# GpSimd's indirect transfers in rows of at most four, and one group's root and two tiles' scatters moved

## What is computed

```python
x = _layernorm(x + _L0_attn_ref(x, L0_attn_w_qkv, L0_attn_w_conv1), axis=-1)
x = _layernorm(x + _L0_ffn_ref(x, L0_ffn_gate_w, L0_ffn_W1, L0_ffn_W2, L0_ffn_Ws1, L0_ffn_Ws2), axis=-1)
# in _L0_ffn_ref, D = 256, H = 192, E = 8 experts, K = 2 per token:
scores = jax.nn.softmax((xf @ gate_w.T).astype(jnp.float32), axis=-1)
top_vals, top_idx = jax.lax.top_k(scores, K)
...
h = jnp.einsum('td,ehd->teh', xf, W1)
y, g = jnp.split(h, 2, axis=-1)
eo = jnp.einsum('teh,edh->ted', y * jax.nn.silu(g), W2)
z = jnp.einsum('te,ted->td', w_dense, eo)
z = z + _gated_mlp(xf, Ws1, Ws2)
```

## Time and profile before

| | us |
|---|---|
| median of 3 runs | 339.32 |
| lowest and highest run | 338.72, 341.7 |
| profiled execution | 339.15 |
| its span, first to last instruction | 337.4 |
| mean granted clock of TensorE | 0.98 of full speed |

### The profile page before, as it was taken

One profiled execution on the slowest core, in us unless ns is written; L12 is line 12 of the kernel. 1 busy time (PEld: TensorE's weight loads), 2 busy tenths in 40 slices (PEclk: granted clock), 3 DMA queues, 4 the chain that ended last, 5 costly groups with the idle time before them and its releaser, 6 DMA issues.

```text
span 337.4 us, 7796 instructions
## 1 busy us (share of the span) xinstructions
PE 311.0 (92%) x2190; PEld 277.4 (82%) x2190; DVE 266.3 (79%) x1083; ACT 194.8 (58%) x442; POOL 205.2 (61%) x241
## 2 busy tenths in 40 slices
PE   3889799999999999999999999999999999999960
PEld 2456688769798879888889999999999999998850
DVE  2795679865888898885789877776799889998686
ACT  1045686637374646465445666666655588688473
POOL 5049650746768776875757544447576856868760
PEclk9979999899999999999999999999999999999996
DMA  7977420211192111153257544447988988876953
GB/s 227 374 257 258 149 65 0 85 48 65 67 254 70 65 65 67 66 159 119 97 159 249 153 152 131 139 140 166 241 234 218 226 208 198 234 219 182 354 198 124
DMA packets 31383, 54.63 MB, mean 162 GB/s; under 512 B 4880, under 2 KB 22544, under 8 KB 31344
## 3 DMA queue, kind: packets, MB, share of 16 engines
q1 hardware_dynamic: 23136, 29.82, 28.5%
q0 software_dynamic: 8208, 24.32, 25.6%
HBM read 29.73 MB, written 24.40 MB: 160 GB/s over the span
## 4 chain that ended last, share of the span: by engine, by line
PE 54%; DVE 17%; DMA 9%; POOL 8%; ACT 5%; issue 3%; SPq 2%; DVEq 0%; ACTq 0%
PE bank L1129 19%; PE bank L1163 10%; PE bank L1012 8%; POOL rows_in L596 4%; PE bank L1093 4%; DMA stage<-ws_t 4%; PE bank L1036 4%; PE bank L996 3%; DMA x<-rows_out 2%; POOL w1lo L552 2%; PE bank L1143 2%; DVE htlo L1468 2%; DVE xs L1259 2%; DVE mix L1462 2%; DMA rows_in<-x,slot 2%
## 5 line engine op out<-in xcount | busy, mean ns | idle before, releaser
L654 POOL DMA_INDIRECT rows_out<-stage,place x71 | 69.8, 983 | 49.0 <-ACT stage L831 32.5
L596 POOL DMA_INDIRECT rows_in<-x,slot x64 | 64.6, 1009 | 47.0 <-DVE slot L1374 30.5
L1129 PE MATMUL bank<-w1hi,bx 128*128 x284 | 64.0, 346 | 0.2 <-DVE bx L1483 0.2
L1129 PEld LDWEIGHTS bank<-w1hi,bx 128*128 128x128 f32 x284 | 48.3, 188 | 0.7 <-issue 0.7
L811 ACT ACTIVATE stage<-bank 128x384 f32<-128x384 f32 (+1 forms) x36 | 17.5, 487 | 36.6 <-PE bank L1129 36.5
L831 ACT ACTIVATE stage<-bank,weight 128x256 f32<-128x256 f32 x71 | 30.0, 470 | 11.0 <-PE bank L1163 9.5
L1129 PE MATMUL bank<-w1lo,bx 128*128 x142 | 36.3, 336 | 0.0
L1483 DVE TENSOR_TENSOR bx<-bank,bx 128x512 fp32r<-128x512 f32 (+1 forms) x36 | 24.5, 684 | 13.5 <-ACT bx L753 13.1
L1036 PE MATMUL bank<-ws2hi,hthi 128*128 128x256 f32 x96 | 28.7, 299 | 5.0 <-DVE htlo L1468 3.3
L1012 PE MATMUL bank<-xthi,ws1hi 128*128 128x512 f32 x96 | 31.6, 411 | 0.0
L1012 PE MATMUL bank<-xthi,ws1lo 128*128 128x512 f32 x96 | 30.5, 400 | 0.0
(11 more groups left out here) (251 smaller groups left out, 871.9 us busy)
## 6 DMA issues: line engine op xcount, KB each, us to landing
stage<-rows_in SPq DMA_DIRECT2D x71, 133.0 KB, 2.6
xs<-rows_out POOLq DMA_DIRECT2D x12, 512.0 KB, 6.1
xs<-x SPq DMA_DIRECT2D x8, 512.0 KB, 8.3
out<-xs SPq DMA_DIRECT2D x7, 512.0 KB
stage<-w_t SPq DMA_DIRECT2D x8, 384.0 KB, 3.9
rows_in<-clear SPq DMA_DIRECT2D x16, 133.0 KB
rows_out<-stage,place POOLq DMA_INDIRECT x71
stage<-w_t SPq DMA_DIRECT2D x2, 512.0 KB, 3.9
```

The costliest lines, as they stand in the source:

```text
L596: pool.indirect_dma_start(rows_in[0:E * CAP, :], bass.IndirectOffsetOnAxis(slot[:, q * G + t, k:k + 1], 0), x2[q % 2][:, t, :], None).then ...
L654: pool.indirect_dma_start(rows_out[:, :], bass.IndirectOffsetOnAxis(place[:, 2 * j + b:2 * j + b + 1], 0), by[j % 4][:, b * C:(b + 1) * C] ...
L1129: mm = pe.matmul(bank_h[j % 2][:, b, 0:F], bx[j % 2][:, (2 * b + k) * P:(2 * b + k + 1) * P], w[:, bass.ds(e, 1), k, :], start=(a == 0), s ...
```

## The change

Scatters are issued by a helper, two transfers for a tile. In each group two tiles are scattered, then comes something else, then the other two: in groups 0 to 5 the root of group q + 2 (as before in groups 1 to 5; in group 0 it stood behind all eight), in group 6 a wait for the first half of the group's shared result (`s_zev[0]`). In group 7 only tiles 28 and 29 are scattered there; tile 30's two transfers come behind pair 0's results and tile 31's behind pair 2's. In the pair loop `rough_rstd2` of pairs 21, 27 and 31 moves from ahead of the pair's first transfer to behind it.

```diff
+            def scatter(q, t):
+
+                for k in range(K):
+                    pool.indirect_dma_start(
+                        rows_in[0:E * CAP, :], bass.IndirectOffsetOnAxis(slot[:, q * G + t, k:k + 1], 0),
+                        x2[q % 2][:, t, :], None).then_inc(s_sc[q % 2], 16)
+
             for q in range(NG):
                 pool.wait_ge(s_slot, q + 1)
-                for t in range(G):
-                    if t == 2 and 0 < q < NG - 2:
-                        rough_rstd(q + 2)
-                    for k in range(K):
-                        pool.indirect_dma_start(
-                            rows_in[0:E * CAP, :], bass.IndirectOffsetOnAxis(slot[:, q * G + t, k:k + 1], 0),
-                            x2[q % 2][:, t, :], None).then_inc(s_sc[q % 2], 16)
-                if q == 0:
-                    rough_rstd(2)
-                elif q < 5:
+                for t in range(2):
+                    scatter(q, t)
+                if q < NG - 2:
+                    rough_rstd(q + 2)
+                elif q < LAST:
+                    pool.wait_ge(s_zev[0], q + 1)
+                if q < LAST:
+                    for t in range(2, G):
+                        scatter(q, t)
+                if 0 < q < 5:
                     low(5 + q)
...
             for j in range(PAIRS):
                 if j % 2 == 0:
                     pool.wait_ge(s_to, j // 2 + 1)
-                if j in ROUGH:
-                    rough_rstd2(ROUGH[j])
...
                     pool.indirect_dma_start(
                         rows_out[:, :], bass.IndirectOffsetOnAxis(place[:, 2 * j + b:2 * j + b + 1], 0),
                         by[j % 4][:, b * C:(b + 1) * C], None).then_inc(s_st[j % 4], 16)
+                    if b == 0 and j in ROUGH:
+                        rough_rstd2(ROUGH[j])
+                if j in (0, 2):
+                    scatter(LAST, 2 + j // 2)
```

## The result

The changed kernel takes **346.22 us** (median of 4 runs, 344.49 to 348.89), the kernel before, run beside it, 340.51 us (338.72 to 343.9): a ratio of **1.019**, 95% interval [1.0137, 1.0243]. In two later series, each beside runs of the kernel before, the same change gave 1.0163 [1.0114, 1.0212] and 1.0173 [1.0122, 1.0224]. So it is slower, by 1.6 to 1.9%, or 5.7 to 6.6 us. Forecast were 344.7 us, 5.4 us or 1.6% above the 339.32 us shown, with a range up to 346.9; two of the four runs, 347.37 and 348.89, lie above it.

The account below looks back on a forecast made before the run. The prediction took TensorE to bound the kernel, busy in 92% of the span and without slack in the pair loop. Stall 3.5, clock 1.5 and root 0.5 make 5.5 us; 339.15 + 5.5 gives 344.7 us, range 341.7 to 346.9.

Parts of the forecast that it names:

- the sign: Whole kernel: the change makes it slower, beginning at 342.7 us; chance 0.87.
- the mechanism: Pair 8's loads wait for all 64 scatters, tile 31's included, so TensorE idles and its clock falls.
- the clock's term: Behind the gap at pair 8, TensorE's clock falls to 1.2 GHz: 1.5 us lost, bounds 0 and 1.7.
- the stall: At pair 8's transposes, TensorE idles from 194.7 to 198.2 us: 3.5 us, bounds 2.5 and 5.2.
- the root: In pair 31, the moved root delays the second transfer by 0.8 and the end by 0.5 us, bounds 0 and 0.8.
- TensorE has no slack in the pair loop: From 187 to 304 us TensorE is busy 117.00 of 117.00 us, so a pause is not made up later.
- pause given back: Rival: the pair loop's 27 steps behind the stall run faster and recover it, giving 339.7 us; chance 0.05.
- The pair loop delays tile 31 to 190.95 and 192.22: On GpSimd, tile 31's two scatters stand behind pair 2's transfers, the last 12.0 us later than before.
- 2.6 + 0.1 + 0.7 + 2.6 = 6.0 us: Before pair 8's transposes: scatter landing 2.6, SyncE's waits 0.1, second load 0.7 later, load landing 2.6 us.
- Groups 0 and 6 cost 0: Group 0's moved root costs 0 (bounds -0.2 and +1.04 us); group 6's wait on GpSimd costs 0.
- shorter rows of scatters help: Rival: no stall, at best 0.2 us gained from the first root, giving 339.0 us; chance 0.04.
- a stall without the fall: Rival: TensorE stalls at pair 8 but its clock does not fall, giving 343.2 us; chance 0.25.

Follow-up runs that it names:

- after_third: The changed kernel run again, unedited, in a later series: 346.4 us, ratio 1.0163 to the kernel before.
- filled_gap_2: The changed kernel with 60 matmuls of unread result ahead of pair 8's transposes: 343.71 us, ratio 1.0108 to the kernel before.
- g7_only_2: The kernel before with only tiles 30 and 31 deferred behind pairs 0 and 2: 346.21 us, ratio 1.0159 to the kernel before.
- t31_pair3: The changed kernel with tile 31 scattered behind pair 3 instead of pair 2: 350.63 us, ratio 1.0287 to the kernel before.
- after_fourth: The changed kernel run again, unedited, in another later series: 346.32 us, ratio 1.0173 to the kernel before.
- g7_undone_2: The changed kernel with group 7 scattered whole, the rest of the change kept: 340.62 us, ratio 0.9998 to the kernel before.
- g0g6_only: The kernel before with only groups 0 and 6 cut in two, no deferral and no roots moved into the pairs: 340.75 us, ratio 0.9993.
- before_again: The kernel before, unedited, profiled on a chip where it takes 356.6 us in the series: 354.85 us.

## Where the prediction was right, and the step of it that failed

It had the sign, the place and the mechanism. **The step that failed is the clock's term:** 1.5 us, with 1.7 as the upper bound, "0.4 of the 3.4 us lies in the gap". The profile after shows 6.8 us at the lower level, 5.4 of them under work, an estimated 2.7 us; and a second fall near the end, for which the sum had no term. Two smaller terms were mis-sized as well, the stall (3.5 for 3.6 to 3.8) and the root (0.5 for 0.3). The median, 346.22, is 1.5 us above the forecast 344.7, and the profiled execution, 348.89, is 2.0 above the range's upper end; 2.85 of its microseconds lie ahead of everything that changed. The forecast ratio, 344.7 / 339.32 = 1.016, is close to the three measured, 1.019, 1.0163 and 1.0173, in part by luck: 0.5 of the 5.5 us is a term that no time shows, and the others were short by as much or more. Its steps:

- *TensorE has no slack in the pair loop.* Right: 99.00 of 99.00 busy behind the gap; the rival "pause given back" is out.
- *The pair loop delays tile 31 to 190.95 and 192.22.* Measured 191.31 and 192.58 in after_third, 0.36 later; that run began group 7 0.5 us later (first scatter at 171.84, not 171.32).
- *From the last scatter's start to the transposes 2.6 + 0.1 + 0.7 + 2.6 = 6.0 us.* Measured 201.05 - 194.61 = 6.4: landing 2.48, SyncE's first load 0.36 behind it where I had estimated 0.1, the second 0.84 later where I chose 0.7 against the row's 0.85, landing 2.71. **The stall**, forecast 3.5, was 3.81, 3.71 and 3.6: short by 0.1 to 0.3, and it was in my two choices that lay at no row. The stall's upper bound was wrong by its own terms: 192.22 + 2.64 + 0.1 + 0.85 + 3.9 is 199.7, so 5.0 and not 5.2, and the range's end 346.7; the changed kernel's own stalls on this kind of chip, 3.6 to 3.8, stay far below it.
- **The clock**, forecast 1.5. That it falls is shown by every profile of the changed kernel, and what the fall costs by filled_gap_2, which takes it away: 1.8 us in the profile's middle row, 2.6 between the medians. I had put the place of the fall, in the gap, together with a length, 3.4 us, from a row in which TensorE was at work. In the five profiles with the stall these two don't go together:

| run | stall | fell at | TensorE resumed | at the lower level | of it at work | lost (estimate) |
|---|---|---|---|---|---|---|
| after | 3.81 | 199.6 | 201.05 | 6.8 | 5.4 | 2.7 |
| g7_only_2 | 3.60 | 198.7 | 200.32 | 6.8 | 5.2 | 2.6 |
| t31_pair3 | 7.13 | 200.0 | 202.41 | 6.8 | 4.5 | 2.2 |
| after_third | 3.71 | 200.3 | 198.94 | 3.4 | 3.4 | 1.7 |
| after_fourth | 3.61 | 200.1 | 198.90 | 3.4 | 3.4 | 1.7 |

Where the clock fell in the gap it stayed low twice as long; where it fell behind the gap, all of the 3.4 us were under work. Neither case gives 1.5. What decides between them isn't shown. My upper bound, 1.7, was none: a low stretch of 6.8 us stands in no row that I had read. The first and last microseconds of one, g7_only_2:

```profile
198.00:199.00 1.00, 0.00 (x0) 0.00 (x0) 0.00 (x0) 0.00 (x0) 0.65 (x1) 0.86 0.77 263
...
205.00:206.00 1.00, 1.00 (x8) 0.92 (x7) 0.16 (x1) 0.65 (x2) 0.00 (x0) 0.73 0.72 165
```

- **A second fall near the end**, in no term. All five of these profiles have it, beginning at 329.8 to 333.1 and for 3.4 us; of the five others of this kind of chip one has one (g7_undone_2, 322 to 325). From pair 10 to the end the six with it take 117.4 to 118.1 us, of the four without it three 116.6 to 116.9 and g0g6_only 118.2. So it may cost most of a microsecond; that, and whether the stall brings it about, was not tested.
- **The root in pair 31**, forecast 0.5. The transfer behind it moved as worked out: 306.53 to 316.10 is 9.57, against 8.75 for the pair's results (303.63 to 312.38), so 0.82. SyncE's loads behind it moved by less than the 0.5: they go out 6.30 to 6.32 us after pair 31's results begin in the seven profiles with the move, 5.97 to 5.99 in the three without, so 0.3. The chain that ended last now runs through the root, in after:

```profile
314.84 1.06 POOL ln2t L627
316.10 2.51 DMA rows_out<-stage,place
318.69 0.38 SPq L480
```

But nothing shows that the 0.3 us reached the end. The time from pair 10 to the end was, over the ten profiles of this kind of chip, 116.8 (before) to 118.2 us (g0g6_only) without the move and 116.6 (filled_gap_2) to 118.1 (after_third) with it. The landing of `load_last`'s rows, 7.31 us in the profile I read, was 8.08 in after and 8.87 in g0g6_only, so it hides them.
- *Groups 0 and 6 cost 0.* Right where the kernel takes 340 us (0.9993). The rival "shorter rows of scatters help" I priced at 0.2 us from the even pitch on GpSimd. That reading was right for the chip of the profile and wrong as a general one: on one chip of the other kind each cut gave half a per cent, on another the change without the deferral 1.3%, by what isn't shown.

So of the sum, 5.0 us were meant for the middle row of the table, and three profiles of the changed kernel show 5.5 to 6.2 there: 0.1 to 0.3 of the difference is the stall's, 0.2 to 1.2 the clock's. The chance of 0.25 for a stall without the fall went to a case that none of those profiles showed.

## What to carry to other kernels

Before you move a DMA behind later work, look for the semaphore that counts *all* of its kind, not for the tile that it carries: here one wait counts 64 scatters, so pair 8's load waits for the last of them, whichever rows it carries. Work out the last start that is still free (here 188 us: wanted at 194.7, less two landings and two issues) and put the work ahead of it. When a full TensorE gets a gap such as this one, add what its clock loses behind the gap, take it from several falls rather than one, don't combine the place of one with the length of another, and keep the longest in the range. And take a gain of half a per cent from one chip for no more than that.

## What the runs showed of the hardware

- The same program takes 339.7 to 340.5 us in the three series on chips of one kind and 353.4 and 356.6 in the two on others. On the latter, ScalarE stood still for up to 6.0 us at a time (before_again) with no instruction in the profile that releases it.
- TensorE's clock fell in or behind each gap of 3.6 to 3.8 us ahead of pair 8 (four profiles): in two before the engine resumed, at the lower level for 6.8 us, in two after it, for 3.4. With matmuls issued through the gap, 3.52 us of them, no fall followed.
- An indirect transfer was to be seen 2.48 us after its start; SyncE's next load followed 0.36 us later (after).
